# Routing of a perceiver's third and last feed forward in pieces between the units of the tokens before

## What is computed

```python
# third feed forward (L2): 6 experts, best two, and a shared one
probs = sigmoid(xt @ gate_w.T + gate_b)
w, idx = top_k(probs, 2);  w = w / (sum(w) + 1e-8)
y = sum_e ge[:, e] * ((silu(xt @ ew1[e].T) * (xt @ ew3[e].T)) @ ew2[e].T)
x = x + y + (silu(xt @ fc1.T) * (xt @ fc2.T)) @ fc3.T
# last feed forward (L3): 64 experts of width 64, best eight of the biased scores
aff = xt @ centroids.T;  idx = top_k(aff + expert_biases, 8)
w = sigmoid(aff[idx]);   w = w / (sum(w) + 1e-8)
x = x + sum_e cw[:, e] * (silu(xt @ W_up[e]) @ W_down[e]) + silu(xt @ Ws_up) @ Ws_down
```

## Time and profile before

| | us |
|---|---|
| median of 3 runs | 5342.03 (5341.34 to 5345.02) |
| profiled execution, its own time | 5361.74 |
| its span, first to last instruction | 5359.9 |
| TensorE busy in it | 4734.5 (88%) |
| VectorE, ScalarE, GpSimd busy | 3211.2, 2103.3, 1840.9 |
| mean granted TensorE clock | 0.929 |

### The profile page before, as it was taken

One profiled execution on the slowest core, in us unless ns is written; L12 is line 12 of the kernel. 1 busy time (PEld: TensorE's weight loads), 2 busy tenths in 40 slices (PEclk: granted clock), 3 DMA queues, 4 the chain that ended last, 5 costly groups with the idle time before them and its releaser, 6 DMA issues.

```text
span 5359.9 us, 138432 instructions
## 1 busy us (share of the span) xinstructions
PE 4734.5 (88%) x48761; PEld 3740.5 (70%) x48761; DVE 3211.2 (60%) x9501; ACT 2103.3 (39%) x5231; POOL 1840.9 (34%) x2796
## 2 busy tenths in 40 slices
PE   4999999999999998995929999777999989977999
PEld 3777777789867776773617777665677768865776
DVE  4777777756556665564425665774566657764333
ACT  1444444422234444220305555332355545532333
POOL 2555555511013333334043433970144334420000
PEclk8999999999989999996959999897999988877999
DMA  6000000000000000000210100002211000005665
GB/s 199 18 18 18 18 18 19 16 1 1 1 25 30 29 31 16 0 0 28 72 55 29 35 31 24 0 0 63 53 32 35 31 13 0 0 0 103 146 145 134
DMA packets 112436, 199.69 MB, mean 37 GB/s; under 512 B 13315, under 2 KB 54659, under 8 KB 111259
## 3 DMA queue, kind: packets, MB, share of 16 engines
q1 hardware_dynamic: 108147, 188.67, 13.2%
q0 software_dynamic: 4096, 8.40, 0.5%
HBM read 183.29 MB, written 18.97 MB: 38 GB/s over the span
## 4 chain that ended last, share of the span: by engine, by line
PE 75%; DVE 8%; issue 6%; ACT 5%; POOL 3%; SPq 1%; DMA 1%; another core or an unknown queue 1%; POOLq 1%; DVEq 0%; ACTq 0%
PE psum_banks L3089 7%; PE psum_banks L555 6%; PE psum_banks L3098 6%; PE psum_banks L560 5%; PE psum_banks L620 4%; PE psum_banks L664 3%; PE psum_banks L671 3%; PE psum_banks L1623 3%; PE psum_banks L624 3%; PE psum_banks L1658 2%; PE psum_banks L2103 2%; PE psum_banks L1084 2%; PE psum_banks L2770 2%; PE psum_banks L1599 2%; ACT scratch L1741 1%
## 5 line engine op out<-in xcount | busy, mean ns | idle before, releaser
L787 DVE TENSOR_REDUCE scratch<-psum_banks 128x2 f32<-128x514 f32 x768 | 531.5, 692 | 400.3 <-PE psum_banks L555 396.3
L706 ACT ACTIVATE scratch<-psum_banks 128x512 f32<-128x512 f32 x768 | 458.7, 597 | 490.9 <-PE psum_banks L565 479.7
L560 PE MATMUL psum_banks<-scratch 32*128 32x128 f32 x6144 | 638.9, 309 | 8.1 <-ACT scratch L706 6.1
L555 PE MATMUL psum_banks<-scratch 32*128 32x257 f32 x3072 | 569.7, 436 | 50.8 <-DVE scratch L788 50.6
L560 PEld LDWEIGHTS psum_banks<-scratch 32*128 32x128 f32 x6144 | 476.2, 185 | 17.4 <-ACT scratch L706 8.6
L3098 PEld LDWEIGHTS psum_banks<-w_L_ffn_down,scratch 128*128 128x128 f32 (+1 forms) x2560 | 335.9, 192 | 165.2 <-issue 140.7
L555 PEld LDWEIGHTS psum_banks<-scratch 32*128 32x128 f32 x3072 | 252.4, 187 | 269.6 <-issue 171.6
L3145 ACT ACTIVATE scratch<-psum_banks 128x512 f32<-128x512 f32 x344 | 205.4, 597 | 483.6 <-PE psum_banks L3089 483.6
L3089 PE MATMUL psum_banks<-scratch,w_L_ffn_up 128*128 128x512 f32 (+1 forms) x752 | 383.2, 605 | 7.4 <-DVE scratch L3260 5.1
L3260 DVE TENSOR_TENSOR scratch<-scratch 128x512 f32<-128x512 f32 x304 | 210.3, 692 | 294.2 <-ACT scratch L3145 272.6
L565 PE MATMUL psum_banks<-shift_T,own_batch 32*128 32x128 bf16 x3072 | 351.1, 214 | 0.0
(11 more groups left out here) (479 smaller groups left out, 12378.2 us busy)
## 6 DMA issues: line engine op xcount, KB each, us to landing
scratch<-route_T SPq DMA_DIRECT2D x136, 512.0 KB, 7.1
scratch<-in_ctx SPq DMA_DIRECT2D x99, 514.0 KB, 3.5
scratch<-in_ctx_rows SPq DMA_DIRECT2D x130, 128.0 KB, 2.0
scratch<-route_T SPq DMA_DIRECT2D x8, 1024.0 KB, 8.0
expert_rows<-in_ctx SPq DMA_DIRECT2D x10, 512.0 KB, 17.7
scratch<-expert_rows SPq DMA_DIRECT2D x16, 192.0 KB, 2.7
expert_out<-scratch SPq DMA_DIRECT2D x16, 192.0 KB, 2.1
w_L_ffn_up<-in_L_ffn_up SPq DMA_DIRECT2D x1, 2992.0 KB
```

The costliest lines, as they stand in the source:

```text
L555: return pe.matmul(S[:, g % 2, :], qbd[q, t.odd, (s // 2) * P:(s // 2 + 1) * P], kT_of[q, t.odd, s // 2, :], start=True, stop=True)
L560: return pe.matmul(W[:, g % 2, c * P:(c + 1) * P], kT_of[q, t.odd, b, c * P:(c + 1) * P], qbd[q, t.odd, b * P:(b + 1) * P], start=True, st ...
L706: act.activation(pT[:, b % 2, 2 * h:2 * h + 2].rearrange("p t c q -> p t (c q)"), W, ACT.Exp).then_inc(exp_ready.sem, 1)
L787: dve.tensor_reduce(parts[:, r.t.odd, 2 * h:2 * h + 2, 0, b], S, X_AXIS, ALU.max, negate=True)
```

## The change

L2 and L3 are built by a new function, `routed_by_features`; L0 keeps the old one. It issues the same operations for a chunk, but only chunk 0 is routed before the units. The pieces of chunk c+1 stand behind named units (`at`, counted from 0 in each chunk) of chunk c. The choice's arrays get memory of their own, the transposes of tokens share one PSUM bank in place of two (bank 0; the scores lie in bank 1; the transposed weights take both), and the normalised, transposed tokens a ring of two chunks. The core of the diff, with the parts that are as before left out:

```diff
-                stages.append(by_features(k, "L2", ...))
+                stages.append(routed_by_features(k, "L2", ...))
-                stages.append(by_features(k, "L3", ...))
+                stages.append(routed_by_features(k, "L3", ...))
+def routed_by_features(k, kind, up_w, down_w, router, router_b):
+    AT = {"L2": {"norms": (0, 1), "x": (3, 4), "route": 5, "shift": 5, "exp": 6,
+                 "choose": (7, 9), "turn": 10, "stats": 11},
+          "L3": {"norms": (0, 3), "x": (5, 8), "route": 10, "shift": 11, "exp": 13,
+                 "choose": (14, 34), "turn": 35, "stats": 36}}[kind]
+    XT, R, TW, Y = k.bank[0], k.bank[1], k.bank[0:2], k.bank[6:8]
+    def sp(sp):
+        for q in range(G * NQ):
+            if q % (2 * NQ) == 0:
+                c = g // 2
+                sp.wait_ge(taken.sem, taken.at(c + 1))
+                sp.dma_start(table[...], weights_T...).then_inc(stored[c].sem, 16)
+                sp.wait_ge(stored[c].sem, stored[c].at(16))
+            if q >= 3:
+                sp.wait_ge(h_done.sem, ...)
...
+        def turn_x(g):
+            pe.wait_ge(xn.sem, xn.at(g + 1))
+            if g % 2:
+                pe.wait_ge(xT_read.sem, xT_read.at(g))
+            elif g:
+                pe.wait_ge(taken.sem, taken.at(g // 2))
...
+        turn_x(0)
+        turn_x(1)
+        route(0)
+        turn_weights(0)
+        for u in range(NU + LAG):
+            if u < NU:
+                ups(u)
+                c, at = divmod(u, 2 * C)
+                if c + 1 < CHUNKS:
+                    if at in AT["x"]:
+                        turn_x(2 * c + 2 + AT["x"].index(at))
+                    if at == AT["route"]:
+                        route(c + 1)
+                    if at == AT["turn"]:
+                        turn_weights(c + 1)
+            if u >= LAG:
+                downs(u - LAG)
...
+        for u in range(NU):            # ScalarE
+            gate(u)
+            c, at = divmod(u, 2 * C)
+            if c + 1 < CHUNKS:
+                if at in AT["x"]:
+                    take_x(2 * c + 2 + AT["x"].index(at))
+                if at == AT["exp"]:
+                    exp(c + 1)
+                if at == AT["turn"]:
+                    take_weights(c + 1)
...
+        some(stats(0), CT)             # VectorE; some(steps, n): n steps of a generator
+        some(normalised(0), CT)
+        some(stats(1), CT)
+        shift(0)
+        some(choose(0), 40)
+        for u in range(NU):
+            g, c = units[u]
+            hidden(u)
+            if c == LAG and g:
+                add_y(g - 1)
+            n, at = divmod(u, 2 * C)
+            if n + 1 < CHUNKS:
+                if at == AT["norms"][0]:
+                    norms = normalised(n + 1)
+                if AT["norms"][0] <= at <= AT["norms"][1]:
+                    some(norms, 3 if gated else 2)
+                if at == AT["shift"]:
+                    shift(n + 1)
+                if at == AT["choose"][0]:
+                    choice = choose(n + 1)
+                if AT["choose"][0] <= at <= AT["choose"][1]:
+                    some(choice, 2 if gated else 1)
+                if at == AT["stats"] and n + 2 < CHUNKS:
+                    some(stats(n + 2), CT)
```

More of the change, by code:

```diff
@@ L3327, in perceiver @@
             if name == "L2_ffn":
-                stages.append(by_features(k, "L2", "L2_ffn_up", "L2_ffn_down", "L2_ffn_gate_w", "L2_ffn_gate_b"))
+                stages.append(routed_by_features(k, "L2", "L2_ffn_up", "L2_ffn_down", "L2_ffn_gate_w", "L2_ffn_gate_b"))
             if name == "L3_ffn":
-                stages.append(by_features(k, "L3", "L3_ffn_up", "L3_ffn_down", "L3_ffn_centroids", "L3_ffn_expert_biases"))
+                stages.append(routed_by_features(k, "L3", "L3_ffn_up", "L3_ffn_down", "L3_ffn_centroids", "L3_ffn_expert_biases"))
             if name == "L2_xattn":
```

249 lines of the change are left out of this document (added).

## The result

| | before | after |
|---|---|---|
| median of the runs, us | 5343.52 (5341.34 to 5350.19, 4 runs) | 5292.34 (5280.78 to 5294.46, 4 runs) |
| ratio, 95% interval | | 0.9898 (0.9881 to 0.9915) |
| profiled execution, us | 5361.74 | 5294.46 |
| stage 9 (L2) in it, us | 216.5 | 202.2 |
| stage 12 (L3) in it, us | 562.2 | 519.3 |

The account below looks back on a forecast made before the run. Bound by an engine-hopping chain in routing and by full TensorE in units. L2: 39.55 - 0.9 - 10.5 - 9.9 - 6.3 = 12.0; L3: 55.0 - 0.9 - 10.5 - 0.4 = 43.2; together 55.2, so 5342.0 to 5286.8 us, range 5269 to 5305.

Parts of the forecast that it names:

- Units start earlier: Routing of chunks 1 to 3 leaves the front: units start 39.55 us earlier in L2, 55.03 in L3.
- One bank: Chunk 0's second four token transposes wait for the first copy: 0.9 us per stage, 1.8 in all.
- TensorE's pieces: Two turn_x, route and weight transposes between units cost their whole length: 3.5 us a chunk, 21.0 in all.
- The pause in L2: TensorE waits at turn_weights behind unit 10 for VectorE's choice: 3.3 us, three times, 9.9.
- The clock: TensorE restarts at the low clock after each L2 pause: 2.1 us lost, three times, 6.3.
- The rival in which the clock holds: No clock loss at L2's pauses: 5280.5 us, or 5270.6 without the pause; chance 0.2, 0.05 of it without.
- Spread weights in time: L2's next weights land 23.6 us after ups(7), before hidden(14) needs them: cost nothing, high end 5.5 a chunk.
- L3: ScalarE's table-load detour makes gate(14) 2.05 us late; 0.13 sticks out of the cover, 0.4 for three chunks.
- Table loads with a drain: Six ScalarE detours in L2 and L3 cost 16.6 us, time 5303.4; table-loads rival's chance 0.1.
- The other side: TensorE's clock falls at all 24 inserted pieces: 50.4 us at 2.1 each, time 5330.9; chance 0.02.

Follow-up runs that it names:

- the last experiment: Middle order plus chunk 0's second four token transposes put into bank 7, in both stages: stage 9 187.4 us, stage 12 518.8, ratio to the kernel before 0.9860.
- middle order: Changed kernel with L2's turn_x, route, shift, exp and choice one unit earlier, turn_weights still behind unit 10: stage 9 188.3 us, ratio to the kernel before 0.9865.
- doubled route: Changed kernel with the route of chunks 1 to 3 run twice over: stage 9 211.0 us, stage 12 524.9 us.
- The two later orders: Changed kernel with L2's weight transposes behind unit 12 or 11 in place of 10: stage 9 212.0 us and 194.9 us.
- L2 alone: Kernel before with only L2 built by the new function, L3 as before: stage 9 202.3 us, stage 12 562.2, ratio 0.9976.
- one-table: Changed kernel with Silu for the exponential of chunks 1 to 3, so no table loads between units: stage 9 198.2 us, stage 12 518.6.

## Why the prediction was right

The two stages gave what was forecast by the mechanism forecast, term by term:

- *Units start earlier* (39.55 and 55.03). Right: it is the whole source of the gain, and each stage's shows alone.
- *One bank*, 0.9. Right: from the start of the stage to the end of the choice it is 3605.15 - 3586.93 = 18.22 us, against 17.24 before; the last experiment gives it back.
- *TensorE's pieces*, 3.5 a chunk. Right: 3.05 - 2.61 = 0.44 for a turn_x, 4.40 - 2.61 = 1.79 for the route, and 0.87 for turn_weights at the full clock (from 3664.86 to 3665.73 in the middle order). The doubled route confirms it in L3.
- *The pause in L2*, 3.3 forecast, 2.90 found, three times. The chain begins where it was put, 1.49 us after ups(7) (1.50), and ends at 10.6 in place of 11.1. The term was oversized by 0.4: hidden's second product and what follows it overlap a little, 3642.90 to 3644.24 being 1.34 where twice 0.72 was counted.
- *The clock*, 2.1 forecast, 1.5 to 1.7 found. The price was taken from the product at 3680.40, before which TensorE had been idle for longer, 5.11 us. The rival in which the clock holds was wrong for these pauses.
- *Spread weights in time*. Right for the order as it is, but with little to spare. For chunk 1 the first load was issued at 3653.83 and landed 8.5 us later, 23.6 us after ups(7) as forecast. For chunks 1 to 3 these loads landed 1.6, 1.2 and 0.3 us before the product of hidden(14) that reads them; the third took 9.3 us in place of 8.5. The two later orders show what comes when the margin is gone.
- *L3*, 0.4 forecast for the table loads. TensorE has no wait of 0.25 us or more between its units, but without the loads the stage is 0.7 shorter, so the term was a little small.
- *Table loads with a drain*, the rival for which the Trainium skill (ScalarE: Activation LUTs, What ACT_TABLE_LOAD costs) speaks: wrong here. The load starts 0.02 us after the gate before it, the exponential 0.01 us after its load, and the gate 0.02 us after the second (which ends at 3638.22 + 1.28 = 3639.50, with the gate at 3639.52). The load itself is 1.28 us, as the page has it.
- *The other side*. The clock did not fall at any inserted piece of the changed kernel. But the rival was less remote than its 0.02 said for L2: with twice as many short matmuls it happened in two of three chunks.

Stage 9 gave 14.3 for 12.0 forecast, stage 12 42.9 for 43.2. With the measured sizes in place of the forecast ones the sums are 39.55 - 1.0 - 10.6 - 8.7 - 4.9 = 14.4 and 55.0 - 1.0 - 10.6 - 0.7 = 42.7, so no large term is missing.

The whole time fits less well. The stages' 57.3 is 6 more than the medians' difference of 51.2. It is inside that difference's interval (45 to 64), and the remainder is put down to the scatter of the other stages, which is not shown. The forecast of 55.2 lies between the two; with a scatter of this size, how near it came to the medians is partly luck. One sentence of the prediction is wrong, though the forecast does not rest on it: that a profiled run is some 20 us above the median of its kernel. The changed kernel's is 2.1 above, and that of L2 alone is 11.5 below; the 19.7 of the kernel before is near the 18.3 by which its stage 6 is longer in the profile.

## What to carry to other kernels

When serial set-up is spread between the units of a full engine, its gain is the chain that disappears from the front, less every piece that the full engine runs; ask for each piece when its *last* input is ready and who stands behind the wait. A piece placed too late moves the wait to the next link (here store and load), one placed too early waits for its own input, and the right slot can be one unit wide: work out both distances before choosing it. Here moving the tokens' transposes, the route and the choice ahead by one unit, with the weights' transposes left where they were, removed every pause between units and was worth 13.9 us of a stage of 202.2. Where other stages scatter by more than the term looked for, measure the changed stage, not the program.

## What was not expected of the hardware

A pause of TensorE of 2.0 to 2.9 us went with 3.41 us at the lower clock in eleven of the twelve pauses of the changed, the L2-alone, the one-table and the doubled-route kernel. The low stretch began between 0.7 us before TensorE went on and 1.4 after, so 1.3 to 1.7 us were lost; at the twelfth, one of 2.04 us, the clock stayed at full. Waits of 0.5 to 1.1 us between units cost nothing beyond themselves. Waits of 3.3 to 3.6 us went with 6.8 us at the lower clock in all three chunks, about 3 us lost in each. And 3.5 us of uninterrupted matmuls of six columns were followed by the lower clock in two of three chunks, while 1.75 us of them were not. The low stretch behind the same wait is not always as long either: behind the first spread weights of L2 the low stretch was 10.2 us long in one kernel and 6.8 in the others, with the same code there. The same stage 6, with the same operations, took 334.5 to 336.3 us in five profiles and 352.3 to 355.4 in six, in the nine experiments by the chip; what makes the difference is not shown.
